# A node update of a graph network: GpSimd writes twice the row into the result, and the row's buffer is loaded anew before its block is finished

## The reference, cut to what matters

```python
u0 = (einsum('eu,ev,uvw->ew', x0, a0, wu000) + INV_SQRT3 * einsum('euk,evk,uvw->ew', x1, a1, wu110)) / sqrt(fan0)
u1 = (einsum('eu,evk,uvw->ewk', x0, a1, wu011) + einsum('euk,ev,uvw->ewk', x1, a0, wu101)) / sqrt(fan1)
ud0, ud1 = _lin(x0, x1, lu0, lu1)
out = node_features + _merge(u0 + ud0, u1 + ud1)     # what the layer returns
x = _layernorm(x + out, axis=-1)                     # what the whole network does with it
```

## Time and profile before

| what | us |
|---|---|
| median of 3 runs | 26809.61 |
| profiled execution | 26817.98 |
| its span | 26815.9 |
| PE busy | 20099.6 (75%) |
| DVE busy | 19989.9 (75%) |
| ACT busy | 11977.1 (45%) |
| POOL busy | 12176.7 (45%) |

### The profile page before, as it was taken

The page is one execution under the profiler, slowest core; times in us unless marked ns, Lnnn a source line. Parts: engine busy times, 40 slices in busy tenths (PEclk is TensorE's granted clock), DMA queues, the critical chain, the costliest instruction groups (busy, mean ns, idle before and its releaser), DMA issues. The chain is left out here.

```text
span 26815.9 us, 474867 instructions
## 1 busy us (share of the span) xinstructions
PE 20099.6 (75%) x102170; PEld 15503.3 (58%) x102170; DVE 19989.9 (75%) x70096; ACT 11977.1 (45%) x39978; POOL 12176.7 (45%) x11987
## 2 busy tenths in 40 slices
PE   1566566664798898888988988973777787777788
PEld 1223222223677777777777777762555676555677
DVE  8333688883688888888888888876777666777666
ACT  0233344443566666666666666653333222333222
POOL 2777655551344444444444444432777101777200
PEclk6677788887788888888888888876999898999888
DMA  0566555553222222222222222222222100222200
GB/s 32 149 172 172 125 111 111 109 110 87 78 73 73 73 73 73 73 73 73 73 73 73 73 73 73 73 69 65 61 61 61 18 5 20 61 60 60 28 5 5
DMA packets 1781692, 1962.59 MB, mean 73 GB/s; under 512 B 754160, under 2 KB 1457344, under 8 KB 1780992
## 3 DMA queue, kind: packets, MB, share of 16 engines
q0 software_dynamic: 565056, 1310.16, 18.5%
q1 hardware_dynamic: 1216576, 651.75, 10.6%
HBM read 1399.54 MB, written 561.06 MB: 73 GB/s over the span
## 5 line engine op out<-in xcount | busy, mean ns | idle before, releaser
L1445 PE MATMUL e_sums<-e_feat,e_same 128*128 128x272 f32 x13824 | 3442.0, 403 | 1360.1 <-ACT e_feat L1466 1237.2
L1427 POOL DMA_INDIRECT e_rows<-x,e_take x3456 | 3618.9, 1047 | 1122.6 <-issue 1045.8
L977 POOL DMA_INDIRECT e_srow<-src_table,e_take x1620 | 1557.5, 961 | 5316.6 <-issue 5126.8
L1445 PEld LDWEIGHTS e_sums<-e_feat,e_same 128*128 128x128 f32 x13824 | 2594.4, 192 | 2207.4 <-issue 1596.4
L581 PE MATMUL e_sums<-e_feat,e_same 128*128 128x480 f32 x3456 | 1965.0, 724 | 1331.1 <-DVE e_feat L649 1331.1
L1012 PE MATMUL e_ps_m<-ident,e_m 128*128 128x128 f32 x12960 | 2333.4, 308 | 554.7 <-DVE e_m L1208 411.2
L565 POOL DMA_INDIRECT e_rows<-table,e_take x1728 | 1876.6, 1086 | 1381.0 <-issue 1351.6
L1012 PEld LDWEIGHTS e_ps_m<-ident,e_m 128*128 128x128 f32 x12960 | 1592.8, 159 | 1240.0 <-DVE e_m L1208 764.5
L581 PEld LDWEIGHTS e_sums<-e_feat,e_same 128*128 128x128 f32 x3456 | 801.9, 244 | 2494.1 <-issue 2407.6
L1026 PEld LDWEIGHTS e_ps_x<-ident,e_lg 128*128 128x128 f32 x12960 | 2188.0, 238 | 76.3
L1026 PE MATMUL e_ps_x<-ident,e_lg 128*128 128x128 f32 x12960 | 2143.5, 321 | 0.0
(11 more groups left out here) (306 smaller groups left out, 52898.4 us busy)
## 6 DMA issues: line engine op xcount, KB each, us to landing
e_pay<-pay_rows SPq DMA_DIRECT2D x432, 470.0 KB, 3.8
order_keys<-key_row SPq DMA_DIRECT2D x810, 128.0 KB
e_keys<-key_row SPq DMA_DIRECT2D x1620, 64.0 KB, 2.8
e_rows<-x,e_take POOLq DMA_INDIRECT x3456, 2.6
order_feat<-in_attr_T SPq DMA_DIRECT2D x810, 64.0 KB
comb<-n_comb SPq DMA_DIRECT2D x300, 164.0 KB, 1.9
e_rows<-table,e_take POOLq DMA_INDIRECT x1728, 4.1
pay_rows<-order_stage,order_put POOLq DMA_INDIRECT x1620
```

The costliest lines, as they stand in the source:

```text
L977: pool.indirect_dma_start(out=srow[t.j][:, :], out_offset=None, in_=src_table, in_offset=bass.IndirectOffsetOnAxis(ap=takes[0][t.j][:, :], ...
L1427: pool.indirect_dma_start(out=rows[t.j][:, q, :], out_offset=None, in_=x, in_offset=bass.IndirectOffsetOnAxis(ap=take[t.j][:, q:q + 1], ax ...
L1445: ins = pe.matmul(sums[b][q // G][:, 512 * h:512 * h + HALF], same[b][:, q, :], feat[b][:, q, h * HALF:(h + 1) * HALF], start=q % G == 0, ...
```

## The change

Before, DVE reads `row` and the accumulated sum `ps_l` in one instruction. After, GpSimd writes `row + row` into `y` behind its copy of `acc`, once the row has landed and once `y`'s last user (block t-2) is through; DVE then adds `ps_l` to `y`. With that, the last reader of `row` is `vector_products`, which ends one DVE step before line 1748 ran. SP's wait before the load changes from `upd_set` of block t-2 to `reduced` (both reductions of block t-2) and `doubled` (GpSimd's instruction of block t-2). SP's steps are peeled for two turns instead of one.

```diff
                     if b.exists():
                         if b.reuses(2):
-                            sp.wait_ge(upd_set, b.count(-1))
+                            sp.wait_ge(reduced, b.count(-2, 2))
+                            sp.wait_ge(doubled, b.count(-1))
                         sp.dma_start(row[b.j][:, 0:D], x[bass.ds(b.t() * P, P), :]).then_inc(row_in[b.j], 16)
...
-                run_steps(sp, step, 2, 2, NB)
+                run_steps(sp, step, 2, 2, NB, peel=2)
...
                     pool.tensor_copy(own[b.j][:, :], acc[:, bass.ds(b.t() * CAT, CAT)]).then_inc(held, 1)
+                    pool.wait_ge(row_in[b.j], b.dma())
+                    if b.reuses(2):
+                        pool.wait_ge(new_set, b.count(-1))
+                    pool.tensor_tensor(y[b.j][:, :], row[b.j][:, 0:D], row[b.j][:, 0:D], ALU.add).then_inc(doubled, 1)
...
                     dve.wait_ge(half_used, b.count(HALVES, HALVES))
-                    dve.scalar_tensor_tensor(out=y[k][:, :], in0=row[k][:, 0:D], scalar=2.0, in1=ps_l[k][:, 0:D],
-                                             op0=ALU.mult, op1=ALU.add).then_inc(upd_set, 1)
+                    dve.wait_ge(doubled, b.count(1))
+                    dve.tensor_tensor(y[k][:, :], y[k][:, :], ps_l[k][:, 0:D], ALU.add).then_inc(upd_set, 1)
```

More of the change, by code:

```diff
@@ L1544, in nodes_update @@
         (wl, ready, scaled, blank, turned, turned_sb, agg_ps, agg_set, z_ps, z_used, reduced, ss_set, vv_set, half_ps, half_sb,
-         half_used, upd_set, squares, roots, new_set, linked, held) = (ph.sem(n) for n in (
+         half_used, upd_set, squares, roots, new_set, linked, held, doubled) = (ph.sem(n) for n in (
              "weights", "ready", "scaled", "blank", "turned", "turned_sb", "agg_ps", "agg_set", "z_ps", "z_used", "reduced",
              "ss_set", "vv_set", "half_ps", "half_sb", "half_used", "upd_set", "squares", "roots", "new_set", "linked",
-             "held"))
+             "held", "doubled"))
         row_in, stored = (ph.sems_of(n, 2) for n in ("row_in", "stored"))
```

## The result

The changed kernel takes 26773.14 us (median of 20 runs), the kernel before 26822.99 us (20 runs): a ratio of 0.9982, 95% interval 0.9975 to 0.9989, some 50 us less. The profiled execution's span is 26793.6 us, against 26815.9, only 22 us less. The two phases themselves, each from its first copy of `acc` to its last `new`, took 1735.1 + 1742.5 = 3477.6 us before and 1704.5 + 1730.4 = 3434.9 us after, 43 us less; the rest of the span, which the change doesn't touch, was 20 us longer in this execution.

The account below looks back on a forecast made before the run. PE's 6.0 us wait for the row load in each block was taken as the bound. A 5.6 us gain less 4.2 us for clock falls, over 96 blocks, gave 134 us: 26675 us, 8 in 10 range 26560 to 26785.

Parts of the forecast that it names:

- its sum: Whole kernel: 96 blocks times 1.4 us gained, 134 us, giving 26675 us.
- the case without change: Each block's clock fall costs 5.0 us plus up to 0.6 for restart: 26752 to 26810 us, chance 0.12.
- The load is early and the 6.0 us wait goes: SP's row load: issued after the second reduction, at 26026.5 instead of 26039.7, so PE's 6.0 us wait per block disappears.
- What is late next is line 696, the root and copy 5: ACT's root before copy 5 waits for DVE's line 696, leaving PE waiting about 2.1 us a block.
- A gain of 5.6 us a block at an unchanged clock: Settled block: 15.63 us from turn_half(1) to contraction 5 becomes 9.94; 5.7 us less 0.1 for DVE's extra semaphore.
- the first rival: PE's clock stays full in settled blocks: all 5.6 us arrive, 538 us in all, 26272 us; chance 0.10.
- GpSimd's doubling at no cost: POOL's added sum beside DVE's first prod: about 0.4 us for 160 columns, costing nothing even at 3.22 us.
- The clock: "with both kinds about 4.2 us on the mean block": PE around the new wait: clock falls to 0.50, costing 3.4 us (6.8 long) or 5.0 (10.0 long).
- the 10.0 us: Length of the clock fall after PE's 2.75 us wait in the phase's last step; priced at 5.0 us.
- The row of 15.6 us: Start of phase n4: PE worked 15.6 us at clock 0.50 without a stop; such a fall costs 7.8 us.
- the rival in which every fall is a long one: Each block pays 5.0 us and up to 0.6 for the restart: 26752 to 26810 us, no change; chance 0.12.
- the third rival: The clock does not come back soon: 15.6 us falls cost 7.8 us, 2.2 above the gain; 27021 us, chance 0.05.

Follow-up runs that it names:

- the run with 16 fillers: The changed kernel with 16 identity transposes that compute nothing ahead of contraction 5, where PE waits for copy 5: 26271.71 us, ratio 0.9789.
- the run with 8 fillers: The changed kernel with 8 identity transposes that compute nothing ahead of contraction 5, where PE waits for copy 5: 26266.44 us, ratio 0.9791.
- both moves and the late load: The kernel before, with the square root put behind copy 5 and columns(0) and columns(1) ahead of turn_half(0): 28018.3 us, ratio 0.9996.

## Why the prediction was wrong

It was right in the direction, in the waits and in the mechanism, and had the size of one term wrong. The measured 26773 us lies in its 8 in 10 range (26560 to 26785), but 98 us above its sum and outside the forecast's own 26580 to 26752. The sum set out from 26809.61 us, the median of 3 runs; the 20 runs of the result put the kernel before 13 us higher, and against these the gain is 50 us instead of 134. A change of no more than 54 us had a chance of 0.13 in the prediction. The wide range holds the measured time only because it took in some of the case without change.

- *The load is early and the 6.0 us wait goes*: right. It is issued 0.3 us after the end of the second reduction.
- *What is late next is line 696, the root and copy 5, with a PE wait of about 2.1 us*: right, 1.9 to 2.1 us.
- *A gain of 5.6 us a block at an unchanged clock*: right. The run with 16 fillers holds the clock and has blocks of 28.5 us, 5.6 less than 34.1; its 26272 us is the time of the first rival.
- *GpSimd's doubling at no cost*: right, 0.45 us against an estimate of 0.4, and the run with the old load shows that neither it nor DVE's further wait costs anything that can be measured.
- *The clock: "with both kinds about 4.2 us on the mean block"*: this is the step that failed, a term that was mis-sized, and it decides. From the settled block lengths the loss is 33.4 - 28.5 = 4.9 us in `n3` and 34.2 - 28.5 = 5.7 us in `n4`. The mean is 5.3 us, so what is left is 0.3 us a block and not 1.4: 29 us in 96 blocks, of the 43 that the two phases got shorter; the rest lies in their first and last blocks. The settled clock is 0.83, and not near the 0.90 of before. The short falls were as forecast: 6.8 us, at a cost of 3.2 us (31.7 - 28.5) against 3.4. The long ones last 17 us and not 10.0, and cost 8.0 us each (36.5 - 28.5) and not 5.0; in `n4` they are every second fall, in the settled part of `n3` 23 of 37.
- *Where the 10.0 us came from.* They were taken from the last step of the phase, which has no messages behind the wait. There the products of `vv`, in which the clock came back, start 7.5 us after the end of the wait; in a long fall of a settled block, with the messages in between, they start 13.8 us after it (26064.13 against 26050.33). The row of 15.6 us would have been the nearer one. The prediction set it aside because messages stand behind the new wait and not the mixture of that row, but the timeline shows that messages stood in those 15.6 us too. The products of the last step and these messages, in the kernel before:

```profile
26799.79 4.51 PE L1617 MATMUL n_ps_s<-ident,n_vv 128*128 128x128 f32 x24
```
```profile
25157.67 2.45 PE L1597 MATMUL n_ps_a<-n_WM,n_accT 128*128 128x160 f32 x8
```

- *The rivals.* The time is that of the rival in which every fall is a long one, but the falls are not alike as that rival had it: in `n4` half cost 3.2 us and half 8.0. The long ones are as the third rival had them (15.6 us at a cost of 7.8), in about every second block and not in all.
- The Trainium skill, page "TensorE: Matmul & The Clock Gate", section "HAM oscillation — how this bites in real kernels", lays such losses to long DMA waits between bursts. This trace does not agree: waits of 1.9 to 2.1 us for a copy bring the clock down in most blocks, and those of up to 1.2 us in the run with 8 fillers in none of the settled ones.

Why just this mixture of falls sets in, one to one in `n4` and with a whole block in between in `n3`, no run here settles.

## What to carry to other kernels

Taking away a wait of PE buys next to nothing while a shorter one stays in its place, if that still brings the clock down: read the granted clock behind the wait and price the fall by what PE does then. The cheapest test is a handful of transposes into a corner of PSUM that nobody reads, put where PE waits; if the clock stays up and the time drops, the next step is real work in their place. Move the waiting instruction (here a square root ahead of a copy) behind what others need sooner.

## What was not expected of the hardware

- Useless work in a wait made the kernel before 0.6% and the changed one 1.9% quicker.
- The same 16 transposes behind the wait and one contraction did not prevent the falls, but cut them, in settled blocks, from up to 17 us to at most 6.8.
- The block of the kernel before sat at 34.1 us with a fall of 6.8 us in each, and the kernel with both moves and the late load fell back to the same 34.1.
- On two other chips the kernel before took 28023 and 28402 us instead of 26823. It has no trace there, but the versions traced there have the longer time outside the two phases: the last layer's edge stage between them takes 2736 and 2799 us instead of 2405. On the first of these chips, the version with both moves and the late load has the two phases at 3480 us, as the kernel before has on its own chip (3478). Ratios over the whole time are a little smaller there for the same gain.
